# Two scatters in flight: how a two-layer attention and expert kernel waits for its indirect writes

## The reference, cut to what matters

```
x = x + xattn0(layernorm(x), ctx)      # 16 heads, masked
h = layernorm(x)
x = x + shared0(h) + experts0(h)       # 64 experts, top 8, capacity 128 rows per expert
x = x + xattn1(layernorm(x), ctx)      # 16 heads, biases
h = layernorm(x)
x = x + shared1(h) + experts1(h) + 0.1 * anchors1(h)   # 32 experts, top 6; one of 16 anchor groups
```

## Time and profile before

| what | us |
|---|---|
| median of 3 runs | 1023.52 |
| lowest, highest | 1021.89, 1030.06 |
| span of the profiled execution | 1134.8 |
| PE busy in it | 947.4 (83%) |
| POOL busy in it | 539.1 (48%) |
| mean granted TensorE clock in it | 0.869 |

### The profile page before, as it was taken

The page is one execution under the profiler, slowest core; times in us unless marked ns, Lnnn a source line. Parts: engine busy times, 40 slices in busy tenths (PEclk is TensorE's granted clock), DMA queues, the critical chain, the costliest instruction groups (busy, mean ns, idle before and its releaser), DMA issues. The chain is left out here.

```text
span 1134.8 us, 23256 instructions
## 1 busy us (share of the span) xinstructions
PE 947.4 (83%) x6378; PEld 690.1 (61%) x6378; DVE 655.0 (58%) x3249; ACT 490.8 (43%) x1606; POOL 539.1 (48%) x545
## 2 busy tenths in 40 slices
PE   5888788777699999768988987867899999998980
PEld 2666566454378787346765655644687767676740
DVE  3676666443245454456877676646565555554578
ACT  2866666444133333115745453311354444444430
POOL 1015555554534445699044444446455545545531
PEclk9999888668899999887979696558899999999965
DMA  9997311003499972753211111366777544444397
GB/s 329 346 372 246 120 63 48 26 11 118 166 293 318 315 234 93 269 212 117 113 67 73 67 72 67 115 272 234 227 223 236 159 134 131 136 139 122 93 370 262
DMA packets 114449, 198.83 MB, mean 175 GB/s; under 512 B 18840, under 2 KB 86765, under 8 KB 111250
## 3 DMA queue, kind: packets, MB, share of 16 engines
q1 hardware_dynamic: 84210, 138.56, 37.3%
q0 software_dynamic: 23040, 50.38, 12.0%
q10 hardware_dynamic: 7072, 8.40, 2.3%
HBM read 114.01 MB, written 98.98 MB: 188 GB/s over the span
## 5 line engine op out<-in xcount | busy, mean ns | idle before, releaser
L985 POOL DMA_INDIRECT buf<-R,RI x240 | 234.7, 978 | 316.7 <-ACT R L1137 137.8
L770 PE MATMUL PS<-R,XT 128*128 x640 | 158.2, 371 | 13.1 <-DVE XT L1608 10.4
L1021 POOL DMA_INDIRECT yb<-YT,DI x99 | 96.3, 973 | 102.6 <-DVE DI L1601 59.4
L1608 DVE COPY XT<-PS 128x256 f32<-128x256 f32 x224 | 94.7, 423 | 77.5 <-PE PS L320 55.5
L315 PE MATMUL PS<-R 128*128 128x256 f32 (+2 forms) x352 | 124.0, 490 | 15.6 <-DMA R<-in_ctxT 10.2
L770 PEld LDWEIGHTS PS<-R,XT 128*128 128x128 f32 x640 | 107.3, 197 | 26.4 <-issue 19.0
L786 PE MATMUL PS<-R,AT 128*128 (+1 forms) x320 | 104.0, 408 | 1.9 <-ACT AT L1318 1.5
L315 PEld LDWEIGHTS PS<-R 128*128 128x128 f32 (+1 forms) x352 | 73.2, 227 | 50.0 <-issue 36.1
L1137 ACT ACTIVATE R<-R,MX 128x120 f32<-128x120 f32 x256 | 80.0, 387 | 41.4 <-DVE MX L1433 31.4
L474 PE MATMUL PS<-C,R 128*120 128x128 f32 x512 | 87.3, 317 | 11.2 <-issue 11.2
L1312 ACT ACTIVATE SL<-PS 128x128 f32<-128x128 f32 (+1 forms) x160 | 42.5, 266 | 114.2 <-PE PS L770 77.1
(11 more groups left out here) (211 smaller groups left out, 1935.8 us busy)
## 6 DMA issues: line engine op xcount, KB each, us to landing
R<-in_ew SPq DMA_DIRECT2D x64, 384.0 KB
BX<-buf SPq DMA_DIRECT2D x128, 140.0 KB
yb<-Z SPq DMA_DIRECT2D x16, 1024.0 KB
R<-yb SPq DMA_DIRECT2D x16, 1024.0 KB, 4.8
R<-buf SPq DMA_DIRECT2D x96, 140.0 KB
R<-in_w SPq DMA_DIRECT2D x8, 1536.0 KB, 10.7
R<-yb SPq DMA_DIRECT2D x8, 1536.0 KB, 10.9
buf<-Z SPq DMA_DIRECT2D x8, 1120.0 KB, 13.3
```

Source lines behind the costliest of these rows:

```text
L770: x = e.matmul(PS[:, 2 + j % 2, 0:2 * wd], XT[:, j % 3, k, :], src[:, bass.ds(regs[j], 1), k * 2 * wd:(k + 1) * 2 * wd].rearrange("p a n - ...
L985: e.indirect_dma_start(out=(buf1 if l else buf0)[:, :], out_offset=bass.IndirectOffsetOnAxis(ap=RI[:, n % 6, k:k + 1].bitcast(U32), axis=0 ...
L1021: e.indirect_dma_start(out=yb[:, :], out_offset=bass.IndirectOffsetOnAxis(ap=DI[:, j:j + 1].bitcast(U32), axis=0), in_=(YTS0 if i < E0 els ...
L1608: e.tensor_copy(XT[:, j % 3, :, :], two(PS[:, j % 2, 0:256])).then_inc(S["d_xt"], 1)
```

## The change

Each scatter gets a number j, counted through both attentions: `first_scatter(l, n) + k`. It adds to semaphore `sc{j % 4}`, of which there are now four. Before it is issued, POOL waits until scatter j - 2 has landed. `scattered(w, l, n)` now waits for the last two scatters of tile n, and SP calls it once, for tile 15, in place of six times.

```
-    + [f"sc{i}" for i in range(6)] + ["z_b0", "z_y0", "z_dum"]
+    + [f"sc{i}" for i in range(4)] + ["z_b0", "z_y0", "z_dum"]
...
+        def landed(w, j):
+
+            if j >= 0:
+                w.wait_ge(f"sc{j % 4}", 16 * (j // 4 + 1))
+
+        def first_scatter(l, n):
+            return K1 * n + K0 * NT if l else K0 * n
+
         def scattered(w, l, n):
 
             if l or n >= 0:
-                s = n % 6
-                w.wait_ge(f"sc{s}", (n // 6 + 1) * 128 if l == 0 else (3 if s < 4 else 2) * 128 + (n // 6 + 1) * 112)
+                j = first_scatter(l, n + 1) if n >= 0 else K0 * NT
+                landed(w, j - 2)
+                landed(w, j - 1)
...
-            for i in range(NT - 6, NT):
-                scattered(w, 0, i)
+            scattered(w, 0, NT - 1)
...
-                    for n in range(NT - 6, NT):
-                        scattered(w, 1, n)
+                    scattered(w, 1, NT - 1)
...
                 for k in range(K1 if l else K0):
                     keep_pace(l)
+                    j = first_scatter(l, n) + k
+                    landed(w, j - 2)
                     e.indirect_dma_start(
...
-                        bounds_check=((DUM_A + 1) if l else E0) * P - 1, oob_is_err=False).then_inc(S[f"sc{n % 6}"], 16)
+                        bounds_check=((DUM_A + 1) if l else E0) * P - 1, oob_is_err=False).then_inc(S[f"sc{j % 4}"], 16)
```

## The result

| | median us | lowest to highest | runs |
|---|---|---|---|
| before | 1023.1 | 1021.89 to 1030.06 | 4 |
| changed | 1101.26 | 1098.63 to 1103.33 | 4 |

The ratio is 1.077, with a 95% interval of 1.0735 to 1.0804: 78 us slower, where 14 were forecast. The profiled execution of the changed kernel took 1101.73, its span is 1100.0, so here page and runs agree.

The account below looks back on a forecast made before the run. It took TensorE (83% busy) to bound the kernel, with scatters costing only at each attention's end. Delays of 5.2 and 8.8 us, counted whole on the 1023.5 median, gave 1037.5 us; own range 1030 to 1045, overall 1012 to 1056.

Parts of the forecast that it names:

- The sign: Whole kernel: the change makes it slower, 1037.5 us against a median of 1023.5.
- the last link: End of each attention: TensorE's first transposition of the expert buffers comes late when the last scatter does; 14.0 us counted.
- Inside the sweeps POOL has room: Scatters within both attentions: POOL idles 317 us, so scatters up to 1 us later per group cost nothing.
- The pace in quiet, 1.39: Scatters in quiet DMA stretches: two take 2.8 us in place of 2.56, so 1.39 each, +0.11.
- Landing and wake-up: Each waiting scatter in quiet: 1.1 us from POOL's end to the landing, then 0.7 until POOL starts again.
- one scatter per 1.2 us: Quiet stretches: with an estimated 2.3 us per transfer and two in flight, the wait costs nothing.
- Full stretches only at the joins: Stretches where weights fill the DMA engines: delays costed at the two attention ends, 5.2 and 8.8 us.
- Tail of the last tiles: Last scatters of the attentions: 5.2 us late at the first end, 8.8 at the second, 14.0 together.
- No cover at the joins: Attention ends: only 5.6 of 14.0 us show in the profile, but plain runs lack that cover, so all 14 count.
- The guards of ACT, DVE and SP: Waits by token tile: SP's shrink, DVE's and ACT's 26 each double; taken as nothing, 8 us as upper end.
- The joins are tighter still: Rival, attention ends: full stretches meet one unbroken POOL burst, 21 us late plus 7, giving 1051.5; chance 0.15.
- The stalls go: Rival, long scatter bursts: waits end other engines' stops, gaining 24 less 5.6 us, giving 1005; chance 0.13.

Follow-up runs that it names:

- e5: The kernel before, unchanged, run and profiled again on a chip where it takes 1021 to 1023 us; profile span 1021.4 us.
- e13: Kernel before, no wait for landings, five small memsets of POOL ahead of each scatter (starts 1.39 us apart): 1025.06 us, ratio 1.0033.
- e19: Kernel before, no wait for landings, two memsets of POOL that wait for each other ahead of each scatter: 1132.67 us, ratio 1.109.
- e16: Changed kernel with the waits only in token tiles 0 to 2 of the first attention: 1017.46 us, ratio 0.9957 to the kernel before.
- e9: The changed kernel, unaltered, timed again beside the kernel before: 1096.37 us, ratio 1.0731.
- e12: Changed kernel with three scatters in flight in place of two, on a chip where the kernel before takes 1022.86 us: 1041.02 us, ratio 1.0211.
- e11: Changed kernel with the waits only in the last two token tiles of each attention: 1034.34 us, ratio 1.0107 to the kernel before.
- e4: Changed kernel with waits in the second attention only, on the chip where the kernel before takes 1129.65 us: 1123.95 us, ratio 0.9945.
- e1: Changed kernel with three scatters in flight, on the chip where the kernel before takes 1129.65 us: 1135.86 us, ratio 1.0035.
- e3: Changed kernel with waits in the first attention only, on the chip where the kernel before takes 1129.65 us: 1135.5 us, ratio 1.0034.
- e15: Changed kernel with waits in the second attention only, on a chip where the kernel before takes 1021.86 us: 1065.14 us, ratio 1.0418.

## Why the prediction was wrong

The sign was right, and so was the last link, that a late last scatter makes TensorE wait for the buffers. Where the lateness is made was wrong, and the size was 14 for 78. Point by point:

**"Inside the sweeps POOL has room", and later scatters there "cost nothing": this step failed.** The room was read from the idle 317 us of the earlier trace rows. It is not room: the row is of the 1130 us sort (in e5 it is 242.6), and 71.4 of that are the one wait ahead of the very first scatter. Room is the supply against the pace. In e5 the first attention's 128 scatters start from 76.4 to 274.9, one per 1.56; the second's 112 from 537.2 to 709.6, one per 1.55. At 1.28 POOL has 0.27 of room per scatter, at 1.39 still 0.16, at 1.63 none; it is at most that much, since in bursts e5's own starts are bound by POOL. So 1.39 costs 3 us (e13), 1.63 would cost an estimated 23, and 2.00 costs 111 (e19). The price of pace has a knee, and the change lies behind it.

**The pace in quiet, 1.39: mis-sized.** 0.97 of issue is right. Landing and wake-up were taken as 1.1 + 0.7; together they take 3.24 - 0.97 = 2.27. By the landing of 752.73, 2.4 after its start, 1.4 to 1.5 of that are the landing and 0.8 the wake-up. So the wake-up, taken from a wait on ACT, was nearly right, and the landing was mis-sized: I had read it from the packets of the queue in the earlier trace rows, and what a wait sees comes some 0.4 later. The +0.35 that results is beyond even the +0.26 that the prediction named for a wake-up of 1.0, and it didn't carry that bound into its sum over all 240 scatters.
The Trainium skill, "DMA: Bandwidth & Descriptors", section on the anatomy of one DMA on the SWDGE path, would put the landing at an estimated 2.3, and the trace agrees with 2.1 to 2.5; what was wrong in the sentence by it, one scatter per 1.2 us, is that the 0.8 from landing to start comes on top.

**Full stretches only at the joins: failed.** I costed those that touch the last tiles, 5.2 + 8.8. The changed kernel meets three: inputs and weights of the start (tiles 0 to 2, 16.6 us late), expert weights (tiles 11 and 12, from 17.8 late at tile 10 to 34.0), FFN weights (tiles 10 to 12 of the second, 46.2 to 68.6). In the second attention 16 us come in the sweep (30.3 late at tile 0, with the first join's delay in it, to 46.2 at tile 9) and 22 in the full stretch. A scatter in it was forecast longer than it is, 3.4: the 14 from 693.5 to 732.1 take 2.8 each.

**The delay stays.** Missing altogether. e16 and e9 have nearly the same delay at tile 2 (19.3 and 16.6), and only the one with the pace of 1.28 makes it good. The long landings make much of the delay and the slow pace keeps it. Neither alone reaches 78 as far as the runs tell: e12, with the long landings and with no wait felt in quiet, but with three in flight, lost 18; the pace in quiet alone is put at 23 by the recipe.

**Tail of the last tiles.** Right in the sum, by luck in part: e11 cost 11.5 us against 14.0, but its last scatter is 10.7 late at the first join where 5.2 were worked out, and TensorE waits 11.96 and 8.66 us there, 8.2 and 4.8 more than in e5, where 5.2 and 8.8 were. (The chain of the second end has slips of its own: 774.4 and 17 x 1.39 make 798.0, not 798.5, and its "270th and 271st" are the 207th and 208th of 240.) The prediction costed two tiles of sixteen.

**No cover at the joins.** Right. e5 has 3.78 and 3.85 us idle before TensorE's first transposition, and its stretch before the first join lacks the stop, as the prediction had argued for the plain runs. The guards of ACT, DVE and SP: nothing, as forecast (e12 has them all).

**The rivals.** "The joins are tighter still" had the mechanism, POOL bound by one long burst, but looked at its last 34 scatters and gave 1051.5. "The stalls go" was false where before takes 1022. Where it takes 1130, e4 came out 0.55% faster and e1 and e3 level in spite of their waits. The sweep whose scatters wait runs there as on the other chips, the sweep whose scatters don't runs slowly: the second attention of e4, to 740, of e15 on one of the other chips, and of e3, all of it:

```profile
572.00:740.00 168.00, 151.71 (x1405) 108.33 (x1405) 147.40 (x788) 87.93 (x313) 81.62 (x84) 0.90 0.36 137
...
539.00:707.00 168.00, 152.29 (x1399) 108.72 (x1400) 147.00 (x784) 87.67 (x312) 82.55 (x84) 0.89 0.36 137
...
573.00:795.00 222.00, 182.20 (x1397) 126.35 (x1395) 150.00 (x790) 88.08 (x315) 109.08 (x112) 0.75 0.32 119
```

TensorE does the same work in 152 us at a clock of 0.90 with the waits and in 182 at 0.75 without. So on that chip this rival has something to it; why the waits help there isn't shown, and the changed kernel itself was not timed there.

## What to carry to other kernels

Before a wait is put on a stream of small transfers, divide the stream's span by its count, over the whole stage and not at its end: that supply interval, against the new interval (issue, landing and wake-up over the number in flight), says whether the stream keeps up; the stream here, at 83% of its supply (1.28 of 1.55), lost next to nothing at 90% (1.39) and 111 us at 129% (2.00). Where landings are sometimes long, ask also whether the stream is fast enough to catch up afterwards. And when the page's span and the median of the runs differ by 11%, the page is of another sort of execution: idle times read from it are not the room of the runs that are timed.

## What the runs showed of the hardware that was not expected

- The kernel before takes 1021 to 1023 us on four chips and 1130 us on a fifth, each within 1% of its median. On that one, and on the page before, the sweeps whose scatters don't wait take 28 to 51 us longer, at a lower granted clock (0.75 for 0.89 in the second), with stops of PE, DVE and ACT that the page of e5 hasn't; where the scatters wait, the second sweep runs as on the others (152 us of PE in 168 on both). The changed kernel took 1096 to 1101 in the three places where it was timed. Why the one chip differs is open.
- From one scatter's start to the start of the one that waits for its landing it takes 3.24 us in quiet: 0.97 of POOL, 1.4 to 1.5 until the landing and 0.8 until the next start.
- POOL's small memsets overlap: one of 10 elements takes 0.12 to 0.14 us alone, five of 8 take 0.26 to 0.31 together and lengthen the interval by 0.11; two of 128 that wait for each other take 0.49 and cost 0.7.
